# Two attention layers for eight images: the end of the kernel in token halves, with a new steady table

## The reference

```
layer 0: h = groupnorm(x) ; q,k,v = W h + b (8 heads of 32 channels)
         w = softmax(q.k * scale over keys) ; a = w v ; y = x + proj(a) + b
layer 1: q = Wq y, k = Wk y (32 rows) ; v = Wv y (256)
         out = gamma * softmax(q.k) v + y
```

## Time and profile before

| | us |
|---|---|
| median of 3 runs | 1545.74 |
| lowest to highest | 1544.25 to 1546.69 |
| the profiled execution | 1541.26 |
| its span, first to last instruction | 1539.4 |
| TensorE busy | 1488.1 (97%) |
| VectorE busy | 1093.1 (71%) |
| ScalarE busy | 747.5 (49%) |
| GpSimd busy | 1196.2 (78%) |

### The profile page before, as it was taken

How to read it: one execution, slowest core, us unless ns; L and a number is a source line. 1 busy time by engine, 2 the same in 40 slices (tenths; PEclk the granted TensorE clock), 3 DMA queues, 4 the chain that set the end, 5 groups by cost and what they waited for, 6 DMA issues and landing times.

```text
span 1539.4 us, 20505 instructions
## 1 busy us (share of the span) xinstructions
PE 1488.1 (97%) x7200; PEld 887.4 (58%) x7200; DVE 1093.1 (71%) x1921; ACT 747.5 (49%) x1372; POOL 1196.2 (78%) x552
## 2 busy tenths in 40 slices
PE   8899999999999999999999999999999999999778
PEld 6454445576555855567555765558555674458247
DVE  4777878767886768877787678867688676665143
ACT  2266455535465255644555354652556435463312
POOL 2199978976999598995989769994989959897804
PEclk8699999999999999999999999999999999999879
DMA  5223040211403033211402114030322113000100
GB/s 149 60 78 84 1 110 22 65 26 49 111 22 83 20 80 83 46 43 55 110 22 65 26 49 110 22 83 22 85 78 45 42 56 83 21 2 14 42 21 28
DMA packets 47143, 85.24 MB, mean 55 GB/s; under 512 B 11072, under 2 KB 21184, under 8 KB 47040
## 3 DMA queue, kind: packets, MB, share of 16 engines
q1 hardware_dynamic: 47040, 83.93, 21.6%
HBM read 18.29 MB, written 8.39 MB: 17 GB/s over the span
## 4 chain that ended last, share of the span: by engine, by line
PE 84%; DVE 6%; SPq 4%; issue 2%; DMA 1%; ACT 1%; POOL 0%; ACTq 0%; DVEq 0%; POOLq 0%
PE st L533 15%; PE work L609 15%; PE pv L564 15%; PE pv L542 14%; PE work L670 7%; DVE mpart L895 4%; PE work L677 3%; PE work L629 3%; PE work L641 3%; SPq L380 3%; PE st L525 2%; PE work L615 2%; PE rec L581 2%; PE work L635 1%; PE rec L586 1%
## 5 line engine op out<-in xcount | busy, mean ns | idle before, releaser
L866 POOL TENSOR_TENSOR acc<-acc,probs 128x1024 f32<-128x1024 f32 x384 | 899.1, 2377 | 35.9 <-ACT probs L744 35.2
L744 ACT ACTIVATE probs<-st 128x512 f32<-128x512 f32 x1152 | 612.1, 602 | 473.3 <-PE st L533 361.4
L895 DVE TENSOR_REDUCE mpart<-work 128x1 f32<-128x512 f32 x1008 | 632.7, 680 | 164.3 <-PE work L609 163.4
L609 PE MATMUL work<-ks,qs 96*128 96x512 f32 x1008 | 421.6, 464 | 12.4 <-DMA ks<-part_hi 3.9
L533 PE MATMUL st<-qs,ks 98*128 98x512 f32 x1024 | 399.0, 435 | 5.3 <-DMA qs<-mrow 3.1
L866 POOL TENSOR_TENSOR acc<-probs 128x1024 f32<-128x1024 f32 x64 | 151.2, 2374 | 188.0 <-ACT probs L744 187.8
L609 PEld LDWEIGHTS work<-ks,qs 96*128 96x128 f32 x1008 | 187.4, 192 | 176.6 <-DVE mpart L895 103.8
L533 PEld LDWEIGHTS st<-qs,ks 98*128 98x128 f32 x1024 | 192.6, 191 | 129.4 <-ACT probs L744 62.5
L542 PE MATMUL pv<-probs,vt 128*32 128x512 f32 x2048 | 252.4, 611 | 0.0
L564 PE MATMUL pv<-probs,l_vt 128*128 128x256 f32 x1024 | 239.6, 382 | 0.5 <-ACT raw L803 0.5
L564 PEld LDWEIGHTS pv<-probs,l_vt 128*128 128x128 f32 x1024 | 192.0, 190 | 35.4 <-ACT probs L744 5.9
(11 more groups left out here) (79 smaller groups left out, 944.1 us busy)
## 6 DMA issues: line engine op xcount, KB each, us to landing
qs<-part_hi SPq DMA_DIRECT2D x120, 128.0 KB, 2.4
ks<-part_hi SPq DMA_DIRECT2D x120, 128.0 KB, 2.4
xa<-in_x SPq DMA_DIRECT2D x16, 512.0 KB, 4.2
y<-in_x SPq DMA_DIRECT2D x8, 1024.0 KB, 5.6
out<-raw SPq DMA_DIRECT2D x32, 256.0 KB, 2.2
qs<-part_lo SPq DMA_DIRECT2D x60, 128.0 KB, 2.4
ks<-part_lo SPq DMA_DIRECT2D x60, 128.0 KB, 2.4
l_qs<-part_hi SPq DMA_DIRECT2D x32, 64.0 KB, 2.0
```

The costliest lines, as they stand in the source:

```text
L609: last = mm(bank, qs[g][0:HI_HI_LO, c, j, tb * P:(tb + 1) * P], ks[g][0:HI_HI_LO, j, half * HALF:(half + 1) * HALF], start=True, stop=True)
L744: nc.scalar.activation(probs[:, n % PRING, half * HALF:(half + 1) * HALF], st[:, (2 * n + half) % ST_BANKS, :], ACT.Exp).then_inc(s_exp1 i ...
L866: pool.tensor_tensor(a, first, probs[:, n % PRING, :], ALU.add).then_inc(s_add0, 1)
L895: last = dve.reduce_max(mpart[:, 4 * j + tb, half:half + 1], bank, AX.X)
```

## The change

- In the last image, GpSimd leaves out the last four adds of the last chunk (key blocks 6 and 7, two pairs each). The sum in the epilogue multiplies `acc` by ones and adds, in the same bank, ones times the four `probs` buffers of these two blocks: 12 matmuls instead of 4.
- The epilogue's QK1 is made and split by token half, each with its own rows transfers (`rows1`). The first half's six go from SP; of the second half's, three go from SP and three from ScalarE, with a semaphore of their own.
- The order of the epilogue: QK1 and two VT1 of the first half follow the last products; then P, QK1 of the second half, four M1 that need only the first half's rows, two VT1, the other twelve M1. The sum of layer 1's last quarter moves behind the last product.
- `STEADY` gets other stops; no entry is added or left out there. `FIRST` and `LAST` are as before.

```diff
 STEADY = {
-    "maxima1": (66, 68, 71, 72, 72, 77, 78, 82, 84, 90, 93, 93, 96, 110, 114, 117, 120, 125),
-    "qk1": (183, 190, 193, 194),
-    "norm": (32, 33, 34, 40, 48, 66, 76, 88, 100, 100, 121),
-    "sums": (8, 14, 14, 19, 26, 62, 62, 74, 93, 96, 128, 131, 152, 152, 153, 153, 153, 153, 155, 156),
-    "sums1": (159, 164, 164, 166, 166, 170, 172, 172, 172, 182, 182, 182),
-    "v0": (178, 190),
-    "layer1": (0, 28, 32, 33, 44, 67, 97, 118, 133),
-    "v1": (14, 35),
+    "maxima1": (65, 65, 67, 70, 75, 77, 83, 85, 87, 88, 93, 93, 94, 111, 113, 113, 115, 125),
+    "qk1": (182, 192, 203, 206),
+    "norm": (32, 35, 35, 41, 49, 63, 64, 97, 100, 109, 109),
+    "sums": (13, 14, 14, 18, 29, 59, 72, 74, 89, 97, 120, 124, 133, 147, 148, 153, 153, 154, 157, 157),
+    "sums1": (159, 159, 160, 162, 166, 166, 170, 172, 173, 176, 176, 177),
+    "v0": (178, 182),
+    "layer1": (20, 35, 35, 35, 49, 70, 104, 113, 134),
+    "v1": (7, 49),
...
 EPILOGUE = {
-    "sums": (2, 2, 5, 5, 5),
-    "layer1": (0, 1, 5, 6, 6, 6, 10, 10, 10),
-    "maxima1": (12, 12, 15, 17, 17, 23, 24, 68, 86, 86, 86, 96, 96, 96, 96, 96, 100, 100),
-    "sums1": (156, 159, 159, 163, 163, 168, 170, 170, 171, 171, 191, 194),
+    "sums": (2, 3, 3, 3, 3),
+    "layer1": (0, 0, 5, 6, 7, 9, 9, 10, 12, 13),
+    "maxima1": (11, 11, 11, 11, 15, 15, 15, 15, 15, 15, 15, 15, 15, 15, 15, 15, 16, 17),
+    "sums1": (157, 157, 157, 163, 169, 169, 169, 186, 190, 192, 195, 195),
 }
...
+    if kind == "epilogue":
+        layer1 = [e for n in range(2) for e in [("P", m, n) for m in range(KT)] + [("QK1", n)] +
+                  [("VT1", 2 * n + q) for q in range(2)]]
+        maxima1 = [("M1", tb, 0) for tb in range(4)] + [e for e in maxima1 if e[0] != "M1" or e[1] > 3 or e[2]]
...
+        LEFT = 2
...
+        def rows1(eng, t, n, done):
+
+            hi, lo = (a[:, 1, 0:HALF].bitcast(F32) for a in (part_hi, part_lo))
+            p0 = 2 * CH * n + CH * t
+            for r, src in enumerate(((hi, hi, lo), (hi, lo, hi))[t]):
+                eng.dma_start((qs1, ks1)[t][CH * r:CH * (r + 1), n * HALF:(n + 1) * HALF].bitcast(F32),
+                              src[p0:p0 + CH, :]).then_inc(done, 16)
...
+                    if kind == "epilogue":
+                        wait_used(sp, ("QK1", 0), kind, b)
+                        rows1(sp, 0, 0, s_stack1)
+                        rows1(sp, 1, 0, s_stack1)
+                        wait_used(sp, ("QK1", 1), kind, b)
+                        rows1(sp, 0, 1, s_half1)
...
-                    pe.wait_ge(s_add0, 14 * n_acc)
+                    pe.wait_ge(s_add0, 14 * n_acc - (2 * LEFT if kind == "epilogue" else 0))
...
+                    if kind == "epilogue":
+                        pe.wait_ge(s_exp0, 2 * L0_UNITS * B)
+                        for blk in range(LEFT):
+                            for j in range(GH):
+                                last = mm(rec[CH * j:CH * (j + 1), :], ones[:, 0:CH],
+                                          probs[:, (SLOTS - 2 * LEFT + 2 * blk + j // 2) % PRING,
+                                                (j % 2) * HALF:(j % 2 + 1) * HALF],
+                                          start=False, stop=blk == LEFT - 1, tile_position=(0, CH * j))
...
-                        pe.wait_ge(s_stack1, 192 * b)
+                        pe.wait_ge(s_stack1, 192 * b - (96 if kind == "epilogue" else 0))
+                    elif (tb, half) == (0, 1) and kind == "epilogue":
+                        pe.wait_ge(s_half1, 96)
...
-                    act.wait_ge(s_add0, ADDS0 * B)
+                    act.wait_ge(s_add0, ADDS0 * B - 2 * LEFT)
+                    wait_summed(act, ("SUM", 1, 1), kind, b)
...
+                    half = slice(2 * CH * e[1], 2 * CH * (e[1] + 1))
+                    nc.scalar.copy(part_hi[half, 1, 0:HALF], bank[half, :]).then_inc(s_hi1, 1)
+                    if e[1] == 1:
+                        wait_used(act, e, kind, b)
+                        rows1(act, 1, 1, s_half1)
...
-                    if blk == 0:
+                    if blk == 0 or (i >= L0_UNITS - 2 * LEFT and b == B - 1):
```

More of the change, by code:

```diff
@@ L45 @@
 STEADY = {
-    "maxima1": (66, 68, 71, 72, 72, 77, 78, 82, 84, 90, 93, 93, 96, 110, 114, 117, 120, 125),
-    "qk1": (183, 190, 193, 194),
-    "norm": (32, 33, 34, 40, 48, 66, 76, 88, 100, 100, 121),
-    "sums": (8, 14, 14, 19, 26, 62, 62, 74, 93, 96, 128, 131, 152, 152, 153, 153, 153, 153, 155, 156),
-    "sums1": (159, 164, 164, 166, 166, 170, 172, 172, 172, 182, 182, 182),
-    "v0": (178, 190),
-    "layer1": (0, 28, 32, 33, 44, 67, 97, 118, 133),
-    "v1": (14, 35),
-    "maxima": places(3, 0, 0, 0, 1, 1, 1, 2, 2, 1, 0, 1, 1, 0, 0, 2, 1, 1, 0, 3, 0, 0, 0, 2, 0, 1, 0, 1, 1, 2, 1,
[6 rows of a table removed]
+    "maxima1": (65, 65, 67, 70, 75, 77, 83, 85, 87, 88, 93, 93, 94, 111, 113, 113, 115, 125),
[6 more added lines that the diff above has]
+    "v1": (7, 49),
+    "maxima": places(0, 2, 1, 0, 1, 1, 1, 2, 0, 0, 2, 0, 0, 0, 2, 0, 1, 2, 0, 1, 0, 0, 0, 3, 1, 0, 0, 1, 2, 0, 2,
[6 rows of a table added]
 }
@@ L259, in attention @@
         s_stack1 = sem("s_l1_stack")
+        s_half1 = sem("s_l1_half")
         s_mc = [[sem(f"s_mc{g}{c}") for c in range(2)] for g in range(GROUPS)]
@@ L456, in step @@
                 if kind == "epilogue" or kind == "last" or kind == "steady":
[L457 to L463, removed]
+                    if kind == "epilogue":
[4 more added lines that the diff above has]
+                        rows1(sp, 0, 1, s_half1)
+                    else:
+                        wait_used(sp, ("QK1",), kind, b)
+                        for n in range(2):
+                            for t in range(2):
+                                rows1(sp, t, n, s_stack1)
                 if kind != "epilogue":
@@ L578, in fill_rec @@
                     n_acc = chunk_no(e, b) + 1
-                    pe.wait_ge(s_add0, 14 * n_acc)
+                    pe.wait_ge(s_add0, 14 * n_acc - (2 * LEFT if kind == "epilogue" else 0))
                     for j in range(GH):
                         last = mm(rec[CH * j:CH * (j + 1), :], ones[:, 0:CH],
-                                  acc[:, c, j // 2, (j % 2) * HALF:(j % 2 + 1) * HALF], start=True, stop=True,
-                                  tile_position=(0, CH * j))
+                                  acc[:, c, j // 2, (j % 2) * HALF:(j % 2 + 1) * HALF], start=True,
+                                  stop=kind != "epilogue", tile_position=(0, CH * j))
+                    if kind == "epilogue":
[6 more added lines that the diff above has]
+                                          start=False, stop=blk == LEFT - 1, tile_position=(0, CH * j))
                 else:
@@ L631, in fill_bank @@
                 elif what == "QK1":
-                    wait_used(pe, ("P", KT - 1, 1), kind, b)
+                    wait_used(pe, ("P", KT - 1, e[1] if kind == "epilogue" else 1), kind, b)
                     for k in range(KT):
-                        for n in range(2):
+                        for n in e[1:] or range(2):
                             last = mm(bank[2 * CH * n:2 * CH * (n + 1), :], wqk1[:, k, :], y[:, k, n * HALF:(n + 1) * HALF],
@@ L774, in use_bank @@
                 elif e[0] == "QK1":
-                    nc.scalar.copy(part_hi[:, 1, 0:HALF], bank).then_inc(s_hi1, 1)
+                    if kind != "epilogue":
+                        nc.scalar.copy(part_hi[:, 1, 0:HALF], bank).then_inc(s_hi1, 1)
+                        return
+                    half = slice(2 * CH * e[1], 2 * CH * (e[1] + 1))
[3 more added lines that the diff above has]
+                        rows1(act, 1, 1, s_half1)
                     return
@@ L925, in use_bank @@
                 elif what == "QK1":
-                    dve.wait_ge(s_hi1, b)
-                    last = dve.tensor_tensor(part_lo[:, 1, 0:HALF], bank, part_hi[:, 1, 0:HALF].bitcast(F32), ALU.subtract)
+                    half = slice(2 * CH * e[1], 2 * CH * (e[1] + 1)) if kind == "epilogue" else slice(0, P)
+                    dve.wait_ge(s_hi1, b + sum(e[1:]))
+                    last = dve.tensor_tensor(part_lo[half, 1, 0:HALF], bank[half, :],
+                                             part_hi[half, 1, 0:HALF].bitcast(F32), ALU.subtract)
                 elif what == "PB":
```

## The result

The changed kernel takes 1525.82 us (median of 4 runs, 1523.86 to 1526.95) against 1545.47 us for the kernel before in the same series: ratio 0.9872, interval 0.986 to 0.9883, that is 19.7 us less (18.1 to 21.6). The forecast was 15.1 less.

The account below looks back on a forecast made before the run. TensorE, busy for 97% of the span, was taken as the bound. End -11.7 us and steady table -3.4 us sum to -15.1: 1530.6 us for the median, range 1521 to 1541.

Parts of the forecast that it names:

- the end: Epilogue, all five steps together: 12.9 us gained up to the last maxima, 1.2 us lost in the tail, -11.7 us.
- the table: Six steady batches: half of TensorE's three open waits goes, -0.55 us a batch, -3.4 us.
- the sign set beforehand for the steady table: Steady batch: about half a microsecond below 179.0 us if right; a period under 178 us would show rival C.
- rival C: Steady batches: the table gives half of the slow stretch's 3.4 us in each, 10.2 us, total 1523.8; chance 0.16.
- step 1: Epilogue sum: without GpSimd's last four adds it starts 9.1 us earlier; its 24 instructions take 3.0 us.
- step 2: Epilogue, layer 1 by token halves: a q/k half takes 1.8 us, a loss of 1.7 us on TensorE over both.
- step 3: Epilogue rows transfers: first six hidden, last six from two queues land at 1472.2; from one queue 1.1 us too late.
- step 4: Epilogue maxima: four run beside the second-half transfers, the last twelve end at 1480.9 instead of 1493.80, 12.9 us gained.
- rival B: End: half clock also over the new dense stretch, 5.1 us less gain, end -6.6, total 1535.7; chance 0.13.
- step 5: Tail: layer 1's last sum behind the last product, so its reciprocals no longer lie beside it, 1.2 us lost.
- D: Steady slots 16-31: VectorE's added load makes TensorE wait, up to 20.4 us, total 1554.4; chance 0.07.

Follow-up runs that it names:

- adds_kept: The changed kernel with GpSimd's last four adds put back and the sum made of acc alone: 1533.1 us, +9.0 us against the changed kernel.
- one_queue: The changed kernel with all six rows transfers of the second token half issued by SP: 1523.6 us, 0.0 against the changed kernel.
- all3: The changed kernel with layer 1's last sum early, three key blocks left to TensorE and small matmuls in the waits: 1518.2 us, -7.7 us against it.
- left3: The changed kernel with three key blocks instead of two left to TensorE, GpSimd's last six adds gone: 1523.8 us, -1.1 us against it.
- awake: The changed kernel with small matmuls that nothing reads where TensorE waits in the epilogue: 1522.7 us, -3.1 us against it.
- load_back: The changed kernel with one value block and layer 1's q/k put back into slots 0-15 of the steady table: 1557.8 us, +33 us against it.

## Why the prediction was right, and where it was off

The total came out nearer than its parts: the end was put 1.2 us too high and the table 4.8 us too low, and these offset one another. That part is luck. By the sign set beforehand for the steady table, a batch under 178 us (it is 177.5), the table did what rival C said and not what the forecast said.

- **The adds (step 1): right in the mechanism.** Forecast 9.1 us for the sum's start; with the adds kept the sum starts 9.2 us later (1453.43 against 1444.27), and adds_kept gives back 9.0 with all that follows. The wait for GpSimd did not vanish: 2.40 us stayed, because the last image's exponentials and projections ended earlier than in the profiled execution before, which had short stretches of half clock there. The projections start 8.2 us earlier, GpSimd's last kept add ends only 5.9 us earlier. The sum took 2.57 us against 3.0 forecast.
- **Token halves (step 2): right.** A q/k half alone took 1.87 us from start to start (1448.69 to 1450.56), against 1.8 forecast, and 1.94 for both halves together before: the edit does double this matmul. The copy of the attention product came behind the q/k half's copy and cost nothing, as forecast.
- **Transfers (step 3): the price of one queue was wrong.** I added the landing's 2.04 us behind the end of the last issue; it counts from the issue's start. With that the six rows from one queue are 5.2 us, not 5.8. The trace of one_queue shows a wait of 0.16 us, not 1.1. One issue of ScalarE took 0.60 us, one of the three 0.79.
- **Maxima (step 4): off by 1.3 us.** From the sum's start to the last maximum I had 30.75 us; it was 32.1. The term that failed is the value blocks at 3.6 us: they ran partly at half clock in the profiled execution. In one_queue, where they ran at the full clock, it is 30.8 us (1443.36 to 1474.15), as forecast. This is rival B in a small form: not over the dense stretch, but behind its end.
- **Tail (step 5): right, and more behind it.** 1.2 us forecast, 1.1 by the timelines of all3 and the changed kernel. Not forecast was the longer half clock, 7.7 us for 4.6, another 1.5 us. Against the forecast's -11.7 the end gave -10.5 (-12.5 to -8.5).
- **The steady table: the term that was mis-sized.** -3.4 us forecast, -8.2 (-10.2 to -6.2) measured. The step said that a shift between stretches is worth nothing in itself and priced only TensorE's open waits. Both failed. The slow stretch gave back 5.7 us, the fast one took 3.5 and the other three 0.7, so a batch fell by 1.5 us where 0.55 was forecast. And the open waits were the wrong rows: they fell by 1.7 us in all, from 7.1 to 5.4, of a gain of 8.0 in the profiles. Most of the gain is time in which TensorE counts as busy, 1068.2 against 1062.5 us, and which waits beside its matmuls became shorter stays open. Rival C had -10.2 for the table, at the edge of the interval, from half of 3.4 us a batch, that is 1.7 against 1.5 measured. Its cause, that TensorE follows VectorE's lighter load, is not shown: in the first stretch VectorE's busy time fell by 3.2 us, but GpSimd's by 2.9 as well. D's cost did not come, although VectorE is now busy for 29.02 of 33.00 us in its stretch.

## What to carry to other kernels

Where one engine is at 97% and its queue is in order, read not its open waits but what lies beside each long entry: a row of matmuls that needs no answer from the second engine belongs beside the second engine's long chain. Taking such entries away cost 19.5 and 33 us here, where the whole new layout is worth 8.2, and a good part of the 33 was the clock behind a wait of 2.3 us. When the last part of a reduction sits on a slow engine and TensorE is idle, give it the last blocks straight from their buffers; here two blocks for 1.6 us of matmuls bought 9 us. In an end that no other work covers, count TensorE's small waits too: the clock was at half behind several of them, and small matmuls put into them held it through the scores (3.1 us gained, with 3 on either side).

## What the runs showed of the hardware that was not expected

- The clock fell to half right after two stretches in which TensorE was busy for 3.06 and 2.81 of 4.00 us, without one long idle time; yet it stayed at 1.00 behind 2.86 and 1.87 of 4.00 us in the same execution, and over the same value blocks in one_queue, adds_kept and left3.
- With small matmuls in the waits it stayed full through the maxima and the scores (awake, all3), where the changed kernel, one_queue, adds_kept and left3 all had half.
- One wait of 2.33 us in load_back's steady part was followed by a granted clock of 0.50 over the whole next stretch of 4 us (804 to 808). The changed kernel's steady part has no such wait and was at 1.00 throughout.
- A matmul of 64 output columns alone takes as long as two beside each other: 1.87 us for 4 instructions against 1.94 for 8.
- The same prologue varies by 2 us between executions: the first exponential came at 53.4 to 53.8 us in some profiles and at 55.3 to 56.1 in others, with nothing changed ahead of it.
